# Seams, norms and fillers laid out anew, and the centring moved into the weights, in a two-layer sequence kernel

## The reference

```python
# layer 0, mixer (a selective scan, 256 inner channels, 16 states)
xd, z = split(x @ W_in.T); xd = silu(causal_conv4(xd) + conv_b)
dt_raw, Bm, Cm = split(xd @ W_x.T); delta = softplus(dt_raw * W_dt + b_dt)
h = exp(delta * A) * h + delta * Bm * xd          # per channel and state, along T
y = (h * Cm).sum(states) + D_param * xd
x = layernorm(x + (y * silu(z)) @ W_out.T)
# layer 0, experts: 16 routed (2 chosen) and one shared, gated by silu
x = layernorm(x + routed(x) + sigmoid(x @ w_share) * shared(x))
# layer 1, mixer: an LSTM of 20 cells along T gives mu_t and sigma_t
w[j, i] = exp(-(i / (j + 1) - mu_j) ** 2 / (2 * sigma_j ** 2)) for i <= j, divided by its norm
x = layernorm(x + w @ x)
# layer 1, experts: 4 layers of 4 experts, 2 chosen of each
for l in range(4):
    xe = layernorm_without_weights(x) * ln_g[l] + ln_b[l]
    x = sum over e of comb[e] * (x + gelu(xe @ w1[l, e] + b1) @ w2[l, e] + b2)
x = layernorm(x + x_at_the_start)
```

## Time and profile before

| | us |
|---|---|
| median of 3 runs (lowest to highest) | 3120.66 (3115.3 to 3121.0) |
| the profiled execution | 3124.14 |
| its span, first to last instruction | 3122.4 |
| PE busy | 2722.2 (87%) |
| DVE busy | 1939.3 (62%) |
| ACT busy | 1388.3 (44%) |
| POOL busy | 1061.9 (34%) |
| mean granted TensorE clock | 0.874 of 2.4 GHz |

### The profile page before, as it was taken

The page is one execution under the profiler, slowest core; times in us unless marked ns, Lnnn a source line. Parts: engine busy times, 40 slices in busy tenths (PEclk is TensorE's granted clock), DMA queues, the critical chain, the costliest instruction groups (busy, mean ns, idle before and its releaser), DMA issues.

```text
span 3122.4 us, 32142 instructions
## 1 busy us (share of the span) xinstructions
PE 2722.2 (87%) x7894; PEld 1308.0 (42%) x7894; DVE 1939.3 (62%) x6569; ACT 1388.3 (44%) x4620; POOL 1061.9 (34%) x913
## 2 busy tenths in 40 slices
PE   4776988889999999899998999888998999999698
PEld 1122553344444444354444444444445444444444
DVE  4857487357774777567765777577766555444422
ACT  3232433335554555445544555455534444444233
POOL 4735258104541445235532455144422001100200
PEclk7587777789996999889997999799989997899699
DMA  3231232003321223113310232123211220121021
GB/s 111 65 86 54 86 101 75 25 13 95 102 71 28 70 88 105 45 33 103 91 61 29 80 108 78 32 71 88 92 34 43 68 62 24 34 61 61 11 81 58
DMA packets 111780, 204.80 MB, mean 66 GB/s; under 512 B 14799, under 2 KB 24422, under 8 KB 111592
## 3 DMA queue, kind: packets, MB, share of 16 engines
q1 hardware_dynamic: 111592, 202.75, 22.2%
HBM read 195.36 MB, written 7.34 MB: 65 GB/s over the span
## 4 chain that ended last, share of the span: by engine, by line
PE 42%; DVE 28%; ACT 14%; issue 7%; POOL 1%; DVEq 0%; POOLq 0%; ACTq 0%
PE p_hid L656 8%; DVE state L1197 7%; PE p_turn L905 6%; PE p_hid L1410 4%; PE p_misc L666 4%; ACT cell_t L919 4%; DVE cell L935 3%; PE p_acc L666 3%; DVE add_c L932 3%; DVE weighed L1206 2%; DVE p_turn L929 2%; ACT decay L1226 2%; DVE hist L940 2%; PE p_gate L465 1%; PE p_hid L955 1%
## 5 line engine op out<-in xcount | busy, mean ns | idle before, releaser
L905 PEld LDWEIGHTS p_turn<-hist,w_hh 22*128 22x128 f32 x2048 | 332.7, 202 | 1023.4 <-DVE hist L940 892.7
L905 PE MATMUL p_turn<-hist,w_hh 22*128 22x4 f32 x2048 | 419.6, 273 | 219.9 <-DVE hist L940 200.9
L656 PE MATMUL p_hid<-xhat,w 128*128 128x512 f32 x1024 | 578.1, 648 | 0.5
L919 ACT ACTIVATE cell_t<-cell 20x4 f32<-20x4 f32 x1024 | 207.7, 203 | 699.4 <-DVE cell L935 699.4
L1135 POOL TENSOR_TENSOR drive<-du,rows 128x512 f32<-128x512 f32 x256 | 470.5, 1838 | 57.7 <-DVE state L1197 42.4
L929 DVE SCALAR_TENSOR_TENSOR p_turn<-p_turn,cell 20x4 f32<-20x4 f32 x1024 | 170.6, 167 | 505.0 <-ACT p_turn L915 484.7
L714 ACT ACTIVATE hid<-p_hid,b1f 128x512 f32<-128x512 f32 x512 | 351.9, 687 | 240.7 <-PE p_misc L666 149.8
L388 POOL TENSOR_TENSOR n_rstd<-n_var,minus_half 128x4 f32<-128x4 f32 x56 | 62.1, 1109 | 1086.7 <-DVE n_var L376 1086.7
L1197 DVE TENSOR_TENSOR_SCAN state<-decay,drive 128x512 f32<-128x512 f32 x256 | 398.0, 1555 | 22.5 <-POOL drive L1139 13.9
L1154 POOL TENSOR_TENSOR y<-y,weighed 128x512 f32<-128x512 f32 x192 | 242.7, 1264 | 439.2 <-DVE weighed L1206 438.8
L1410 PE MATMUL p_hid<-w_gate,mean_w 128*128 128x512 f32 (+1 forms) x630 | 339.8, 627 | 0.0
(11 more groups left out here) (208 smaller groups left out, 3316.2 us busy)
## 6 DMA issues: line engine op xcount, KB each, us to landing
rows<-rows_dram SPq DMA_DIRECT2D x128, 512.0 KB, 5.0
w<-w_dram SPq DMA_DIRECT2D x128, 256.0 KB, 2.6
w<-in_w2T SPq DMA_DIRECT2D x128, 256.0 KB, 2.7
comb_b<-comb_dram SPq DMA_DIRECT2D x64, 512.0 KB, 4.7
rows<-comb_dram SPq DMA_DIRECT2D x128, 128.0 KB, 2.9
w<-in_w1T SPq DMA_DIRECT2D x16, 256.0 KB, 2.7
w_dram<-w SPq DMA_DIRECT2D x16, 256.0 KB, 2.1
out_xT<-result SPq DMA_DIRECT2D x8, 256.0 KB, 2.5
```

The lines of the kernel that those rows point to most:

```text
L656: nc.tensor.matmul(p_hid[:, v % 2, :], w1[:, v // FB, (v % FB) * P:(v % FB + 1) * P], xhat[:, :], start=True, stop=True).then_inc(g_h, 1)
L905: nc.tensor.matmul(gate_bank(i)[:, :, t:t + 1], w_hh[:, :], before, start=False, stop=False, skip_group_check=True).then_inc(gates_done, 1)
L919: nc.scalar.activation(cell_t[64:64 + PE_, :], cell[32:32 + PE_, :], ACT.Tanh, scale=0.5).then_inc(cell_tanh, 1)
```

## The change

What it does, part by part. **SP:** the loads that the opening doesn't need go into `bulk_sp`, drawn one at a time through chunk 0's scan. **Norms of layer 1's layers:** the mean over features is taken out of the first weights once, in the fold (w1 less its column mean), so that the product of an uncentred x is that of the centred one; only the variance is still formed, as mean square less squared mean, the mean from a fifth column of the router. Sums of squares are over xl itself, by ACT. The combination is transposed and copied in the slots of the first products. **Fold:** ACT scales instead of DVE, PE forms the mean, DVE subtracts. **Scan:** in period 0 too PE sums y; the sum of step k is issued with step k + 1. **Layout:** attention one slot later in all and its inputs in another order, with one DVE operation less; layer 0 with three to four empty slots, starting at slot 1 and resting in a layer's last slot; `decays` ahead of all else in the slot; z products apart. **Fillers:** up to 704 columns (two matmuls), 384 where one product stands beside, and in more slots.

```diff
@@ norm_pe, choose_dve @@
-    def norm_pe(nm, n, src, ready, extra=None, early=None):
+    def norm_pe(nm, n, src, ready, early=None):
...
         nc.vector.scalar_tensor_tensor(out=arg[:, :, :], in0=mid[:, :, :].to_broadcast([P, B, E]), scalar=-0.5,
                                        in1=logit[:, :, 0:E], op0=ALU.mult, op1=ALU.add).then_inc(s_arg, 1)
-
+        yield
...
             mm = nc.vector.match_replace(left[:, j, :], top[:, j, :], logit[:, j, :], 1.1 * NEVER)
         mm.then_inc(s_step, 1)
-        yield
         yield
@@ layer1_pe @@
-    att_slots = lambda q: 17 + q + 1
+    NORM = 5
+    LAYER = NORM + UN + 2
+    att_slots = lambda q: 19 + q
...
-            ln = norm_pe(n1, q * NL + l, src, (n1.src_ready, q * NL + l + 1), logits, (lambda: mean_of_two(n)) if l else None)
...
+            pe.wait_ge(n1.src_ready, q * NL + l + 1)
+            for j in range(B):
+                mm = nc.tensor.matmul(p_hid[:, 0, j * (E1 + 1):(j + 1) * (E1 + 1)], tile(src, j), w_router1[:, l, :],
+                                      start=True, stop=True)
+            mm.then_inc(g_logit, 1)
+            yield
+            pe.wait_ge(n1.square_done, q * NL + l + 1)
...
+            for _ in range(3):
                 yield
+            pe.wait_ge(n1.rstd_done, q * NL + l + 1)
...
-                    if v == 1:
-                        pe.wait_ge(g_combT_taken, n + 1)
...
+                if v == 0:
+                    pe.wait_ge(g_comb, n + 1)
+                    for j in range(B):
+                        mm = nc.tensor.transpose(tile(p_acc1, j)[0:E1, :], comb1[:, j, :], ident[:, :])
+                    mm.then_inc(g_combT, 1)
...
+                    if f == 0 and e == 1:
+                        pe.wait_ge(g_combT_taken, n + 1)
@@ layer1_act @@
+            act.wait_ge(n1.src_ready, q * NL + l + 1)
+            if l:
+                act.wait_ge(n1.var_done, q * NL + l)
+            nc.scalar.activation(n1.square[:, :], src, ACT.Square).then_inc(n1.square_done, 1)
+            yield
+            yield
+            choose_act(n, arg1, tanh1, g_arg, g_tanh)
+            yield
+            yield
+            act.preload_act_table(ACT.Gelu)
+            yield
...
-                    if v == UN - 1 and l < L - 1 and q + 3 < NCH:
-                        act.preload_act_table(ACT.Exp)
+                if v == 1:
+                    act.wait_ge(g_combT, n + 1)
...
+                    nc.scalar.copy(combT1[:, :], p_acc1[0:E1, :]).then_inc(g_combT_taken, 1)
+                if v == UN and l < L - 1 and q + 3 < NCH:
+                    act.preload_act_table(ACT.Exp)
@@ layer1_dve @@
-        nc.vector.tensor_scalar(mw[:, 1, :], p_hid[:, 1, :], 0.0, 1.0 / T, ALU.max, ALU.mult).then_inc(mup_taken, 1)
...
+        nc.vector.scalar_tensor_tensor(out=mdrive[:, :], in0=p_hid[:, 0, :], scalar=0.0, in1=mdrive[:, :],
+                                       op0=ALU.max, op1=ALU.add).then_inc(mup_taken, 1)
...
+        mu_scan((0, 1))
+        yield
+        mu_scan((2, 3)).then_inc(mu_done, 1)
...
+            yield
+            next(ch)
+            nc.vector.tensor_copy(mean1[:, :], p_hid[:, 0, 0:B * (E1 + 1)].rearrange("p (b e) -> p b e", b=B)[:, :, E1:E1 + 1]
+                                  .rearrange("p b o -> p (b o)")).then_inc(mean_step, 1)
+            next(ch)
...
+            nc.vector.tensor_tensor(mean1[:, :], mean1[:, :], mean1[:, :], ALU.mult).then_inc(mean_step, 1)
+            yield
...
+            nc.vector.scalar_tensor_tensor(out=n1.var[:, :], in0=p_acc1[:, 448:448 + B], scalar=EPS, in1=mean1[:, :],
+                                           op0=ALU.add, op1=ALU.subtract).then_inc(n1.var_taken, 1)
+            next(ch)
+            yield
+            next(ch, None)
+            yield
+            dve.wait_ge(n1.rstd_rows, q * NL + l + 1)
+            nc.vector.tensor_tensor(xhat[:, :], src, p_misc1[:, :], ALU.mult).then_inc(n1.out_done, 1)
@@ mamba_pre_pe @@
-    PRE = 11
+    PRE = 10
...
+        z(0, p_acc1)
         yield
...
         mm.then_inc(ssm_done, 1)
         yield
+        z(1, p_misc1)
         yield
@@ mamba_scan_pe @@
+            if early and k:
+                sum_y(k - 1)
+            yield
+            yield
+        if early:
+            sum_y(NS - 1)
@@ fold_pe, fold_dve, fold_act @@
+            pe.wait_ge(fold_grown, k + 1)
+            if k:
+                pe.wait_ge(fold_scaled, k)
+            nc.tensor.matmul(p_misc1[:, :], mean_w[:, :], w1[:, k % E1, :], start=True, stop=True).then_inc(fold_mean, 1)
...
-            nc.vector.tensor_scalar(w1[:, k % E1, :], w1[:, k % E1, :], ln_g[:, k:k + 1], None, ALU.mult).then_inc(fold_scaled, 1)
+            nc.vector.tensor_tensor(w1[:, k % E1, :], w1[:, k % E1, :], p_misc1[:, :], ALU.subtract).then_inc(fold_scaled, 1)
...
+            act.wait_ge(folded, k + 1)
+            nc.scalar.activation(w1[:, k % E1, :], w1[:, k % E1, :], ACT.Copy, scale=ln_g[:, k:k + 1]).then_inc(fold_grown, 1)
@@ fillers @@
-    L0_AT = 4
+    L0_AT = 1
+    BURST = {LAYER - 1: 1, 0: 1, 1: 2, 2: 2, 3: 2}
...
+    L0_WIDE = {1, 5, 7, 46, 48, 52, 54} | set(range(11, 44))
+    FILL = (704, 384, 0)
+
+    def filling(i, slot, o, wide, done, last):
+        if i == 0 and done["leave"] == 0:
+            wide += done["scan"] % 2
+            return (p_misc1 if done["fold"] > 52 else p_acc1[:, L * UN:]), FILL[wide] if not 45 < done["fold"] <= 52 else 0
+        if done["pre"] >= 10 or (last and i and slot >= att_slots(i - 1) + L * LAYER + 5):
+            return p_hid[:, 1, :], FILL[wide]
...
+        if slot < att:
+            wide += slot < 4 or 8 <= slot < 8 + q or slot == 9 + q
+            return p_acc1 if slot < 8 else p_hid[:, 1, :], FILL[wide]
+        if slot < tail and 0 <= o <= 3:
+            return p_hid[:, 1, :], CT >> wide
@@ period @@
-        early = False
+        early = i == 0
...
+            if u < NCH and layer1 and att - 1 <= slot < tail - 2:
+                for _ in range(BURST.get(o, 0)):
+                    next(burst, None)
             if layer1:
                 next(layer1, None)
...
+            last = layer1 is not None and att < slot < tail and o == LAYER - 1
+            wide = 0
+            if layer0 and not ((heavy or last) and slot < CH) and slot >= (L0_AT if layer1 else 0):
                 next(layer0, None)
...
-                    for _ in range({22: 1, 0: 2, 1: 2, 2: 2, 3: 1}.get(o, 0)):
-                        next(burst, None)
@@ opening, start of PE @@
+                if k >= 4 and k % 2 == 0:
+                    next(bulk, None)
...
+                pe.wait_ge(mz_taken, 3 * NB)
+                pe.wait_ge(dt_taken, 3 * NB)
```

More of the change, by code:

```diff
@@ L586, in layer1_pe @@
         pe.wait_ge(xm_done, min(q + 3, NCH))
[L587 to L590, removed]
+        for k, g in enumerate((0, 2, 1, 3)):
+            if k >= 2:
+                pe.wait_ge(mup_taken, q * 4 + (k - 1))
+            nc.tensor.matmul(p_hid[:, k % 2, :], w_mub[:, g, :], hist[:, q % 2, :, :], start=True, stop=True).then_inc(mup_done, 1)
             yield
@@ L613, in layer1_pe @@
         mm.then_inc(ss_summed, 1)
-        for _ in range(6):
+        for _ in range(7):
             yield
@@ L630, in layer1_pe @@
             src = x3[:, :] if l == 0 else xl[:, l % 2, :]
[L632 to L636, removed]
-            ln = norm_pe(n1, q * NL + l, src, (n1.src_ready, q * NL + l + 1), logits, (lambda: mean_of_two(n)) if l else None)
[L639 to L645, removed]
-                yield
+            pe.wait_ge(n1.src_ready, q * NL + l + 1)
[6 more added lines that the diff above has]
+            for j in range(B):
+                mm = nc.tensor.matmul(p_acc1[:, 448 + j:449 + j], tile(n1.square, j), mean_w[:, 0:1], start=True, stop=True)
+            mm.then_inc(n1.var_done, 1)
+            for _ in range(3):
+                yield
+            pe.wait_ge(n1.rstd_done, q * NL + l + 1)
+            for j in range(B):
+                mm = nc.tensor.matmul(tile(p_misc1, j), n1.rstd[:, j:j + 1].to_broadcast([P, P]), ident[:, :],
+                                      start=True, stop=True)
+            mm.then_inc(n1.rstd_rows, 1)
+            yield
             pe.wait_ge(n1.out_done, q * NL + l + 1)
@@ L689, in layer1_act @@
             yield
-        for _ in range(9):
+        for _ in range(10):
             yield
@@ L696, in layer1_act @@
             n = q * L + l
[L697 to L708 removed]
+            src = x3[:, :] if l == 0 else xl[:, l % 2, :]
+            act.wait_ge(n1.src_ready, q * NL + l + 1)
[9 more added lines that the diff above has]
+            yield
             for v in range(UN + 2):
@@ L892, in layer0_pool @@
         yield from norm_pool(n0, 2 * q)
-        for _ in range(6 + 3 * U0):
+        for _ in range(9 + 3 * U0):
             yield
@@ L969, in mamba_pre_pe @@
         yield
+        taps(0, (2, 3))
         yield
-        taps(0, (2, 3))
         yield
@@ L1158, in mamba_scan_pe, with sum_y @@
         pe = nc.tensor
```

(10 more changed lines are left out.)

226 lines of the change are left out of this document (115 added, 111 removed).

## The result

The changed kernel takes 3140.94 us (median of 6 runs, 3136.6 to 3153.4) where the kernel before took 3119.57 beside it (3114.3 to 3121.0): ratio 1.0083, 95% interval 1.0061 to 1.0105. It is 0.8% slower; I had forecast 3018. The profiled execution took 3142.3 us with a span of 3140.5, 18.1 more than before.

The account below looks back on a forecast made before the run. Bound: a PE-ACT-DVE ring of LSTM steps, 1.62 us each, plus side work queued between steps. Terms -13 - 20 - 57 - 9 - 4 = -103 from 3124.1 give 3021, less 3.5: 3018 us; 8 in 10 range 2955 to 3085.

Parts of the forecast that it names:

- Opening, -13: Before period 0: ssm stored earlier, fewer PE and DVE waits, less a later start(); -13 us, bounds -18 and -5.
- Period 0, -20: Period 0: POOL additions and DVE scalings go, PE, ACT and DVE work comes; -20 us, bounds -35 and +10.
- booked at -8: Period 0, 32 slots after scan and fold: without POOL's addition a pair falls from 4.54 to 4.0 us; gain 8.
- The 4 us that I hung on it: Period 0: if POOL never blocks the DVE subtraction, the period would end some 4 us earlier than the sum.
- The seams, -1.6 a layer: Layer 1's norms, four per period: 27.2 us become 25.6; -1.6 a layer, -6.5 a period, bounds 0 and -3 a layer.
- logits now wait for xl: Layer 1's norms: the wait and PE work make two slots 5.4 us together, PE-bound, where they were 4.0 and 3.1.
- rival C: PE's clock comes back whole in periods 1 to 7: -45 us beyond the forecast, 2973 us; chance 12%.
- D: At 1.2 GHz long fillers outlast slots and products queue; period 0 also slower: +122 us, 3140; chance 7%.
- Heads and tails, -2.5 and -2.5 a period: Period heads: one DVE operation fewer, fillers from slot 0, -2.5; layer 0's end: no DVE wait, work spread, -2.5.
- B: PE becomes the bound: longer fillers show in some 40 filled slots a period, 42 us come back, 3060; B or E 21%.
- E: Norms' slots stay as long because DVE takes over, heads as well: 57 shrinks to 12, 3063 us; B or E 21%.
- Last chunk, -4: Last layer-1 chunk alone: waits and centring go, logits and mean squared take most back; -4 us, bounds -8 and -1.

Follow-up runs that it names:

- e2_cover: Changed kernel plus two 512-column fillers at each layer 1 seam, behind a layer's last product and ahead of the wait for xl: 3057.1 us, ratio 0.9800.
- e7_l0last: Changed kernel with layer 0 drawn on in a layer's last slot, as in the kernel before, and no more fillers: 3107.1 us, ratio 0.9943.
- e10_l0at4: Changed kernel with both seam fillers, no fillers in slots 0 to 3 of periods 1 to 8, layer 0 beginning at slot 4: 3019.8 us, ratio 0.9685.
- e4_w512: Changed kernel with its fillers of 704 and 384 columns cut to 512 and 256, as in the kernel before: 3139.8 us, ratio 1.0068.

## Why the prediction was wrong, point by point

*Opening, -13: -14.6.* In the other runs the same opening takes 9 to 17 us less than before. POOL's first drive starts at 39.91, right behind its own chain, and the first scan at 41.56 (forecast: near 42; before: the earlier trace rows):

```profile
22.65 0.58 ACT L1072 COPY ssm<-p_hid 33x512 f32<-33x512 f32 x1 [1.24 <-PE p_hid L1038]
23.25 0.34 SPq L1087 DMA_DIRECT2D rows_dram<-ssm  x1
...
39.91 1.26 POOL L1185 TENSOR_TENSOR drive<-du,rows 128x512 f32<-128x512 f32 x1
...
41.56 2.19 DVE L1254 TENSOR_TENSOR_SCAN state<-decay,drive 128x512 f32<-128x512 f32 x1 [4.22 <-POOL drive L1189]
```

*Period 0, -20: -5.6* in the profiled execution, about -12 in most of the experiments (314 us). The fold and scan slots behaved: slots 16 to 47 went from 105.7 to 95.6 us. The first 16 grew by 6.6, and that term I had booked as a gain: PE does 9.8 us more in them, at a clock of 0.75. The next 32, booked at -8 because POOL no longer adds to y, gave nothing: 73.1 us against 72.6, half of it (slots 48 to 63) at a clock of 0.83. Three rows of the changed kernel:

```profile
311.90:366.40 54.50, 52.50 (x170) 31.33 (x170) 24.35 (x104) 24.75 (x73) 11.99 (x14) 0.75 0.23 74
366.40:462.00 95.60, 89.23 (x294) 45.67 (x294) 78.17 (x203) 42.20 (x149) 25.48 (x32) 0.94 0.35 108
462.00:535.10 73.10, 64.21 (x198) 33.44 (x199) 56.17 (x168) 27.62 (x125) 25.68 (x27) 0.91 0.23 76
```

The subtraction took 0.686 to 0.690 us in all 16 places, never the 1.49 that I had kept as its other price. But POOL worked beside it in only six of them, for 0.31 us once and 0.03 us otherwise; the scaling of the earlier trace rows had 1.4 us of POOL beside it each time that it took 1.49. The page SBUF — State Buffer of the Trainium skill says, in its section Who interferes with whom, that a DVE operation with at most one SBUF input and outside the two-port modes does not contend with GpSimd. The trace does not contradict it and hardly tests it. The 4 us that I hung on it were not there to gain: my sum had the subtraction at 0.69 already.

*The seams, -1.6 a layer.* The working of it held at the clock it was worked for. The first seams went from 21.6 to 19.5 us on average (-2.2). In e2_cover the two slots for which I had 5.4 together mostly take 2.5 and 3.0, and the next two, for which I had 3.0 and 2.9, take 2.7 and 2.5 to 2.9; its seams of period 4 take 19.9 to 20.6 where the kernel before took 21.2 to 21.6, all at clock 1.00. (My sum was off by itself: its parts, 7.1 to 5.4, 5.3 to 5.9 and 0.9 for the table load, make 2.0 a layer, not 1.6.) **The step that failed** stands in the sentence "logits now wait for xl": I added up what PE does in those slots and made them PE-bound, and did not ask what PE does while it waits. It idles 2.3 us in two slots, and in the changed kernel those two take 2.8 and 5.4 us and the next 5.1, because the same list of work runs at 1.2 GHz and takes nearly twice as long. Nor did I price that layer 0 rests in the last slot: by e7_l0last that rest alone carries 34 us of the 84 that the two fillers give back. I priced the clock only as a gain (rival C) or as a loss in period 0 (D). The Trainium skill, TensorE: Matmul & The Clock Gate, Part 1, which I cited for C, says that idleness throttles; I used it for the fillers, which take idleness away, and not for the new wait, which adds it. The seams agree with it (1 of 21 at clock 1.00 with the idle stretches, 17 of 21 with them filled); the 34 us at the turn to period 4, in the last section, do not. My sum had some -29 for these 21 seams (1.6 each in periods 1 to 5, 1 for period 6, 1.3 each in period 7), measured is +43.6, and keeping the clock brings it to -35.

*Products between, part of the -1.6:* -21.8 us over 28 layers, 0.8 each, with the table load (0.9) out of the gelu's slot.

*Heads and tails, -2.5 and -2.5 a period (about -28 with period 7's 3 us): +30.6.* This term was mis-sized, not only its clock. I had the fillers beginning at slot 0 at a net gain and counted no PE work in the head; the row of period 4 shows 16.5 us more. Slots 0 to 3's fillers are 16 of the heads' 56.5, layer 0 at slot 1 between 22 and 35; 5 us are left in e10_l0at4, which still has the extra slot. The tails give 26 back.

*Rivals.* B: the width of the fillers changed nothing (e4_w512). Filled slots at the end of period 0 are 1.69 us against 1.62, too little for its 42. C: the mean clock rose from 0.874 to 0.887 and bought nothing as a whole. It rose most in period 0 (0.78 to 0.89) and fell in the seams (e.g. to 0.74), where PE had no slack; that this is why is my reading. D named 3140 us, a hair off the measured time, but that is chance: it was to decide where period 0's clock fell under 0.7, and that was 0.89, and the longer fillers cost nothing (e4_w512). Only its picture of a step's product queuing behind a filler at 1.2 GHz was seen, in slots 0 to 3, for 16 us. E: no; the seams' DVE and ACT time is as I had worked it out.

*Last chunk, -4: +1.2.* Not looked into further.

The change with four small edits (e10_l0at4, 3019.8: two fillers where PE would wait, none in slots 0 to 3, layer 0 back at slot 4) comes within 2 us of the forecast and beats both kernels. That it meets 3018 is luck: its seams and products give -72 where I had some -38, its heads and tails -7 where I had -28, period 0 -12 where I had -20, the last chunk +0.9 where I had -4.

## What to carry to other kernels

Here a new wait of TensorE cost more behind it than in it. When a change makes TensorE wait for a result that it used to run ahead of, price the slots behind the wait at 1.2 GHz too, and try unread work in the gap before anything else; here taking work out of the slow slots gave 16 us, filling the gap in front of them 84. Put such work only where the engine would idle: in slots that it fills already it cost 8 to 13 us (the heads) and 17 (the seams of the kernel before). Cut the periods at equal steps before judging: a period's mean clock of 0.91 looked untouched while its worst slots ran at half of it.

## What the runs showed of the hardware

The clock did not follow PE's busy share as I had thought. At the turn from period 3 to 4 PE was busy without a gap, with fillers of 704 columns among its work, and stayed at 1.2 GHz for 34 us. In the seam of the first rows the clock fell at 738.1, behind idle stretches of 0.98 and 0.89 us and 0.1 us into the third, of 1.38:

```profile
737.50:738.10 0.60, 0.38 (x2) 0.29 (x2) 0.32 (x2) 0.58 (x2) 0.35 (x1) 0.96 0.43 106
738.10:751.70 13.60, 12.38 (x31) 7.93 (x32) 6.20 (x38) 5.84 (x16) 0.69 (x1) 0.50 0.15 54
1642.60:1676.70 34.10, 34.10 (x68) 16.32 (x67) 17.72 (x59) 10.02 (x35) 8.50 (x8) 0.50 0.00 1
```

In 18 of the 20 later seams that lost the clock it fell 2.5 to 5.1 us after the seam's start, around the wait for xl; in two it fell within a us of the start, with only the 0.98 behind it. The 0.98 stands in the covered seams of e2_cover too, and there the clock mostly held. In one seam PE idled 0.53, 0.28 and 1.13 us and the clock stayed at 2.4 GHz (2555.0 to 2574.3, above), while with the same three stretches it fell in five others of periods 6 and 7. So the runs show that filling the idle stretches keeps the clock, and not how much idle time loses it; nor does any run tell what ends a low stretch.
